# Cross-attention of a decoder layer: keys and queries interleaved by head, context in four buffers, stacks not cleared

## The reference

```python
q = (x @ Wq).reshape(B, N, HEADS, hd).transpose(0, 2, 1, 3)        # HEADS 16, hd 32
k = (context @ Wk).reshape(B, M, HEADS, hd).transpose(0, 2, 1, 3)
v = (context @ Wv).reshape(B, M, HEADS, hd).transpose(0, 2, 1, 3)
scores = jnp.einsum('bhid,bhjd->bhij', q, k) * scale
scores = jnp.where(context_mask[:, None, None, :], scores, max_neg)
attn = jax.nn.softmax(scores, axis=-1)
out = jnp.einsum('bhij,bhjd->bhid', attn, v)
return out.transpose(0, 2, 1, 3).reshape(B, N, DIM) @ Wo
```

## Time and profile before

| | |
|---|---|
| median of 3 runs | 4101.87 us |
| the profiled execution | 4104.39 us |
| its span | 4102.5 us |
| PE busy | 3330.3 us (81%) |
| DVE busy | 2647.3 us (65%) |
| ACT busy | 2227.0 us (54%) |
| POOL busy | 1061.0 us (26%) |
| DMA packets | 582.43 MB, mean 142 GB/s |

### The profile page before, as it was taken

The page is one execution under the profiler, slowest core; times in us unless marked ns, Lnnn a source line. Parts: engine busy times, 40 slices in busy tenths (PEclk is TensorE's granted clock), DMA queues, the critical chain, the costliest instruction groups (busy, mean ns, idle before and its releaser), DMA issues. The chain is left out here.

```text
span 4102.5 us, 50439 instructions
## 1 busy us (share of the span) xinstructions
PE 3330.3 (81%) x15064; PEld 2553.6 (62%) x15064; DVE 2647.3 (65%) x4397; ACT 2227.0 (54%) x4058; POOL 1061.0 (26%) x1139
## 2 busy tenths in 40 slices
PE   5899999999999996377877778775729989950799
PEld 4687877777787875244554455543518877740587
DVE  5787777777777774555655566565653349977554
ACT  4676767667676763155655555563122224448665
POOL 1233333232323232044544444453300000000000
PEclk9999999999999998688988898897969999985899
DMA  4444443444434432333333333324642237779775
GB/s 128 127 131 124 139 123 124 131 134 120 133 120 129 131 108 70 88 96 93 75 88 91 91 80 87 92 61 162 227 141 92 110 118 265 273 279 410 245 247 194
DMA packets 294941, 582.43 MB, mean 142 GB/s; under 512 B 37672, under 2 KB 119600, under 8 KB 280384
## 3 DMA queue, kind: packets, MB, share of 16 engines
q1 hardware_dynamic: 282048, 554.61, 42.6%
q10 hardware_dynamic: 12672, 25.17, 1.7%
HBM read 339.49 MB, written 172.79 MB: 125 GB/s over the span
## 5 line engine op out<-in xcount | busy, mean ns | idle before, releaser
L1555 DVE TENSOR_REDUCE ca_negm<-ca_mx 128x1 fp32r<-128x512 f32 x512 | 353.2, 690 | 433.2 <-PE ca_mx L1701 426.1
L640 POOL TENSOR_SCALAR sa_ex<-sa_ex,sa_rs 128x512 f32<-128x512 f32 x512 | 356.7, 697 | 952.3 <-DVE sa_rs L518 952.3
L513 DVE TENSOR_REDUCE sa_nm<-sa_st 128x1 f32<-128x512 f32 x512 | 351.1, 686 | 269.3 <-PE sa_st L747 268.2
L704 PE MATMUL sa_pj<-sa_xh,sa_w 128*128 128x512 f32 x1536 | 459.7, 419 | 11.7 <-DVE sa_kl L496 9.8
L389 ACT ACTIVATE sa_eh<-sa_tr 128x512 fp32r<-128x512 f32 x512 | 306.7, 599 | 293.9 <-PE sa_tr L757 290.8
L1628 POOL TENSOR_TENSOR ca_el<-ca_ex,ca_eh 128x512 fp32r<-128x512 f32 x256 | 365.5, 1429 | 164.8 <-ACT ca_eh L1484 163.9
L382 ACT ACTIVATE sa_ex<-sa_st,sa_nm 128x512 f32<-128x512 f32 x512 | 351.2, 686 | 58.2 <-DVE sa_nm L513 54.9
L522 DVE TENSOR_TENSOR sa_el<-sa_tr,sa_eh 128x512 fp32r<-128x512 f32 x512 | 351.2, 686 | 36.9 <-ACT sa_eh L389 30.1
L1476 ACT ACTIVATE ca_ex<-ca_st 128x512 f32<-128x512 f32 x512 | 298.2, 589 | 79.2 <-PE ca_st L1719 78.1
L1731 PE MATMUL ca_ov<-ca_eh,ca_vc 128*66 128x512 f32 x512 | 226.7, 443 | 120.0 <-ACT ca_osb L1491 72.2
L757 PE MATMUL sa_tr<-top_ident,sa_ex 128*128 128x128 f32 x2048 | 309.7, 274 | 0.2 <-POOL sa_ex L640 0.2
(11 more groups left out here) (244 smaller groups left out, 7695.9 us busy)
## 6 DMA issues: line engine op xcount, KB each, us to landing
sa_w<-w_split SPq DMA_DIRECT2D x56, 1536.0 KB, 7.4
up_g<-gate SPq DMA_DIRECT2D x50, 512.0 KB, 4.4
gate<-gate_ev SPq DMA_DIRECT2D x24, 1024.0 KB, 3.8
gate<-up_g SPq DMA_DIRECT2D x48, 512.0 KB, 2.9
up<-up_ev SPq DMA_DIRECT2D x24, 1024.0 KB, 5.6
mul_a<-gate SPq DMA_DIRECT2D x48, 512.0 KB, 12.0
mul_b<-up SPq DMA_DIRECT2D x48, 512.0 KB, 13.0
dn_a<-gate SPq DMA_DIRECT2D x96, 256.0 KB, 3.5
```

Of the source, the lines that this page charges most:

```text
L513: nc.vector.tensor_reduce(nm[:, u % U:u % U + 1], st[:, u % 2], AX_X, ALU.max, negate=True).then_inc(dve_mx, 1)
L640: nc.gpsimd.tensor_scalar(ex[:, u % U], ex[:, u % U], rs[:, u % U:u % U + 1], 1.0, ALU.mult, ALU.mult).then_inc(pool_n, 1)
L704: yield nc.tensor.matmul(pj[:, bank], w[:, n % 2, m, part, k], xx[:, b % 2, k], start=(i == 0 and k == 0), stop=(i == 2 and k == DK - 1))
L1555: nc.vector.tensor_reduce(negm[:, n % 2, qt, h:h + 1], mx[:, m % 2], AX_X, ALU.max, negate=True).then_inc(dve_mx, 1)
```

## The change

Five things, all in the cross-attention stage. (1) The columns of Wq and Wk are permuted within each group when they are split, so that the projection leaves element d of head j on partition 4d + j instead of 32j + d; the four heads of a group then go to their four stacks in one DMA, since partition 4d + j is written to partition d, head j. (2) Keys and queries, mask row and maxima need 8 DMAs a step instead of 32; all of a stack's DMAs count on one semaphore for each place of the ring, and keys are no longer issued at t = 5 and 7 but all at t = 8. (3) Context has four buffers and is loaded at t = 1 of the step before the one that transposes it. (4) The mask of the next batch is loaded before its x. (5) The rings are not cleared; POOL sets the rows of ones, and DVE sets the two columns of ones in vc alone.

```diff
+    STACKS = 16 * 7
-        cr = sp.sb("cr", [P, 2, CD])
+        cr = sp.sb("cr", [P, NT, CD])
+        def columns(tile, n):
+            if CK <= n < 2 * CK:
+                return tile
+            return tile.rearrange("p (g j d) -> p g d j", j=HS, d=XD)
+        def split_columns(tile, n):
+            if CK <= n < 2 * CK:
+                return tile
+            return tile.rearrange("p (g d j) -> p g d j", j=HS, d=XD)
             def load_context(j):
-                if j >= 2:
-                    e.wait_ge(pe_ct, j - 1)
-                e.dma_start(cr[:, j % 2], xs[j]).then_inc(cr_in[j % 2], 16)
+                if j >= NT:
+                    e.wait_ge(pe_ct, j - NT + 1)
+                e.dma_start(cr[:, j % NT], xs[j]).then_inc(cr_in[j % NT], 16)
+            def stack(n, tile, src, part):
+                e.dma_start(f32(tile[part * XD:(part + 1) * XD, n % RING]), f32(src[:, :])
+                            ).then_inc(stacked[n % RING], 16)
+            def stack_keys(n):
+                r = n % RING
                 if n >= RING:
                     e.wait_ge(pe_st, U * (n - RING) + U)
-                for j in range(HS):
-                    e.dma_start(f32(k4[MR:MR + 1, r, j]), env["mask_n"][b:b + 1, :]).then_inc(mask_in[r], 16)
+                e.dma_start(f32(k4[MR:MR + 1, r]), env["mask_n"][n // XG:n // XG + 1, :].partition_broadcast(HS)).then_inc(stacked[r], 16)
+                e.wait_ge(act_kh, n + 1)
+                stack(n, k4, kh, 0)
+                stack(n, k4, kh, 1)
+                e.wait_ge(pool_kl, n + 1)
+                stack(n, k4, kl, 2)
+            def stack_queries(n):
+                e.wait_ge(act_qh, n + 1)
+                stack(n, q4, qh, 0)
+                stack(n, q4, qh, 2)
+                e.wait_ge(dve_ql, n + 1)
+                stack(n, q4, ql, 1)
             def max_rows(n):
                 e.wait_ge(act_mr, n + 1)
-                for j in range(HS):
-                    e.dma_start(f32(q4[MR + 1:MR + 2, n % RING, j]), f32(mrow[j:j + 1, :])).then_inc(mr_in[n % RING], 16)
+                e.dma_start(f32(q4[MR + 1:MR + 2, n % RING]), f32(mrow[:, :])
+                            ).then_inc(mr_in[n % RING], 16)
...
-                if t == 5 and n < N:
-                    stack_keys(n, range(3), 0)
-                    stack_keys(n, range(3), 1)
-                if t == 7 and n < N:
-                    stack_keys(n, range(3), 2)
                 if t == 8 and n < N:
-                    for part in range(3):
-                        stack_keys(n, range(3, 4), part)
-                    mask_row(n)
-                    for j in range(HS):
-                        stack_queries(n, j)
-                if t == 3 and s >= 0 and s % XG == 1 and s // XG + 1 < B:
-                    load_context(NT * (s // XG + 1))
-                    load_context(NT * (s // XG + 1) + 1)
-                if t in (8, 10) and context_tile(s, t - 1) is not None:
-                    load_context(context_tile(s, t - 1) + 1)
+                    stack_keys(n)
+                    stack_queries(n)
+                if t == 1 and s >= 0 and s % XG == 0 and s // XG + 1 < B:
+                    for i in range(NT):
+                        load_context(NT * (s // XG + 1) + i)
                 if t == 9 and s >= 0 and s % XG == 1 and s // XG + 1 < B:
+                    load_mask(s // XG + 1)
                     load_x(s // XG + 1)
-                    load_mask(s // XG + 1)
...
-                nc.scalar.activation(w_hi[:, n], w_raw[:, n % 2], ACT.Copy).then_inc(act_w, 1)
+                nc.scalar.activation(split_columns(w_hi[:, n], n), columns(w_raw[:, n % 2], n), ACT.Copy).then_inc(act_w, 1)
...
-            nc.vector.memset(f32(q4[:]), 0.0).then_inc(zeroed, 1)
-            nc.vector.memset(f32(k4[:]), 0.0).then_inc(zeroed, 1)
-            e.wait_ge(zeroed, 2)
-            nc.vector.memset(f32(q4[MR:MR + 2]), 1.0).then_inc(zeroed, 1)
-            nc.vector.memset(f32(k4[MR:MR + 2]), 1.0).then_inc(zeroed, 1)
-            nc.vector.memset(f32(vc[:]), 1.0).then_inc(zeroed, 1)
+            nc.vector.memset(f32(vc[:, :, :, :, 2 * XD:VW]), 1.0).then_inc(ones_set, 1)
...
+            nc.gpsimd.memset(f32(q4[MR:MR + 2]), 1.0).then_inc(ones_set, 1)
+            nc.gpsimd.memset(f32(k4[MR:MR + 2]), 1.0).then_inc(ones_set, 1)
```

More of the change, by code:

```diff
@@ L42 @@
 WQMAX = 7.0
-ZEROED = 5
+ONES = 3
 BIG = float(2.0 ** 100)
@@ L1273, in cross_attention_stage @@
         dve_w = sp.sem("dve_w")
-        zeroed = sp.sem("zeroed")
-        cr_in = [sp.sem(f"cr_in{i}") for i in range(2)]
+        ones_set = sp.sem("ones_set")
+        cr_in = [sp.sem(f"cr_in{i}") for i in range(NT)]
         xq_in = sp.sem("xq_in")
@@ L1290, in cross_attention_stage @@
         dve_vl = sp.sem("dve_vl")
-        stacked = [[sp.sem(f"stacked{r}{j}") for j in range(HS)] for r in range(RING)]
-        mask_in = [sp.sem(f"mask_in{r}") for r in range(RING)]
+        stacked = [sp.sem(f"stacked{r}") for r in range(RING)]
         pe_mx = sp.sem("pe_mx")
@@ L1358, in load_mask @@
                 e.dma_start(maskb[:, :], env["mask_f"][b:b + 1, :].partition_broadcast(P)).then_inc(maskb_in, 16)
-            def stack_keys(n, heads, part):
+            def stack(n, tile, src, part):
+                e.dma_start(f32(tile[part * XD:(part + 1) * XD, n % RING]), f32(src[:, :])
+                            ).then_inc(stacked[n % RING], 16)
+            def stack_keys(n):
                 r = n % RING
[L1362 to L1371, removed]
@@ L1399, in outputs @@
                             ).then_inc(o_out[j % 2], 16)
-            for i in range(2):
-                load_context(i)
+            load_context(0)
             load_weights(0)
             load_weights(1)
-            for i in range(2, NT):
+            for i in range(1, NT):
                 load_context(i)
@@ L1412, in _ @@
                 load_weights(n)
-            e.wait_ge(zeroed, ZEROED)
+            e.wait_ge(ones_set, ONES)
             for G, s, t in slots():
@@ L1451, in high_key @@
                 if n:
-                    for j in range(HS):
-                        e.wait_ge(stacked[(n - 1) % RING][j], 96 * ((n - 1) // RING) + 96)
+                    e.wait_ge(stacked[(n - 1) % RING], STACKS * ((n - 1) // RING) + STACKS)
                 nc.scalar.activation(kh[:, :], km[:, :], ACT.Copy).then_inc(act_kh, 1)
@@ L1654, in transpose_context @@
                 bank_free()
-                e.wait_ge(cr_in[j % 2], 16 * (j // 2) + 16)
+                e.wait_ge(cr_in[j % NT], 16 * (j // NT) + 16)
                 if j % NT == 0 and j:
@@ L1659, in transpose_context @@
                 for k in range(CK):
-                    last = nc.tensor.transpose(ms[:, cols(k)], cr[:, j % 2, cols(k)], ident[:, :])
+                    last = nc.tensor.transpose(ms[:, cols(k)], cr[:, j % NT, cols(k)], ident[:, :])
                 last.then_inc(pe_ct, 1)
@@ L1715, in scores @@
                 if a % U == 0:
-                    e.wait_ge(mr_in[r], 64 * (n // RING) + 64)
+                    e.wait_ge(mr_in[r], 16 * (n // RING) + 16)
                 if a >= 2:
```

19 lines of the change are left out of this document (4 added, 15 removed).

## The result

The changed kernel takes 3908.72 us (median of 4 runs, 3906.31 to 3914.25), the kernel before, on the same chip, 4103.49 us: ratio 0.9525, 95% interval 0.9509 to 0.9542. The forecast was 3852 us in a range of 3800 to 3940: the side and the range are right, the gain is 195 us where 250 were forecast. The profiled run of the changed kernel took 3914.25 us, its span 3912.2.

What follows compares the result with a forecast made beforehand. No engine was full in cross-attention; waits from SP's issue order bound it. Profiled 4104.4 - 241 (steps) + 28 (x behind stacks) - 37 (start) = 3854, adjusted for a profiled run 2.5 us above the median: 3852 us, range 3800 to 3940.

Steps and rivals of the forecast that it cites:

- The start: Start of cross-attention: no clearing, earlier weight splits, faster first stacks and maxima together save 37 us.
- the 5.4 us of the first fill: Start of the stage: first stacks start once kh is there, flow 6.9 us, land by about 1722, saving 5.4 us.
- The strided weight reads: Weight splits of seven tiles, read with a step of 32 elements: 0 to 9.2 us lost, 2 taken.
- rival B: Weight splits: reading with a step costs four times the duration, giving 3878 us; chance 0.09.
- The context stall: Context steps: PE's 130.2 us of waits for tiles go when loaded a step ahead; such steps become 26.6 us.
- all of them move 227: Stack block in each step: all DMA engines move 227 GB/s, so six stacks, 1.57 MB, take 6.9 us.
- the cover of 0.7 us: Store of t = 12 behind the stacks: lands at 1898.5, ACT wants its buffer at 1899.2, so 0.7 us spare.
- the term of 4 us: Steps that load mask and x behind the stacks: 4 us lost in each of 7, 28 us in all.
- an ordinary step becomes 29.3 - 4.6 = 24.7 us: Ordinary cross-attention steps: ACT's wait of 4.6 us for the store goes, leaving 24.7 us (bounds 22.1 and 29.3).
- the forecast's signs: Cross-attention windows: steps of 24 to 26 us expected; forecast wrong if ordinary steps stay above 27 us.
- A: Store of t = 12: its wait moves from SP's issue into the DMA engines, costing 105, 3957 us; chance 0.13.
- C: Every step's stacks: the fused DMA falls on few engines, making the kernel slower, 4288 us; chance 0.05.

Runs made afterwards that it cites:

- micro: Also written (1): no layer computed, only copies in blocks of 1.57 MB, each awaited; six fused stacks took 11.7 us a block, 134 GB/s.
- keys7: Keys' stacks issued at t = 7 instead of t = 8, against the changed kernel with four output buffers and x ahead of the stacks: 3893.29 us, 0.9491.

## Why the prediction came out as it did

**The start: 33.9 for 37, in part by two misses that cancel.** DVE's first low part comes at 1648.04 (forecast: before 1652), PE's first projection at 1674.37 (near 1677), and putting the clearing back costs 34 us. The projection is 33.0 us earlier, where 29.5 were forecast (the first high part of a weight is itself 3.3 us earlier). What failed is the 5.4 us of the first fill: none of it came. The stacks leave SP by 1684, but the last lands 11 us after its issue: the same drain rate as in the steps. The maxima in one issue gave about 1.3 us for 1.9 (the first maximum tile is 32.6 us earlier, the next step's maxima 33.9).

**The strided weight reads: right.** 1.09 instead of 0.63 us on ACT, 1.05 instead of 0.69 on DVE, 1.7 and 1.5 times, inside the bounds of 1 and 2; rival B, at four times, is out. The Trainium skill's penalty for accesses that leave a 16-byte line (SBUF — State Buffer, section "Door 1: The DMA port swizzle") would give such a cost, and the trace agrees; the cost is small here.

**The context stall: right in its mechanism.** No wait of PE for a context tile is left, and loading it as before costs 84 us.

**The step that failed is "all of them move 227": six fused stacks take 11.7 us, not 6.9.** The forecast read the rate off single stacks at a share of 0.41 and scaled it to a full share. Copies of 128 partitions into 32 are slower in themselves: 134 GB/s alone (1), 137 to 143 in the kernel. By the forecast's own arithmetic the cover of 0.7 us at the store of t = 12 then becomes a lack of 4.1 us. It showed fully in the steps with x: there ACT waits 8.8 to 9.8 us and PE 3.4 to 4.3 for x, and the step takes 32.8 us against 25.9 in the fastest version, so the term of 4 us was in truth 7. The step behind it takes 28.0 us against 26.1, at a granted clock of 0.92 to 0.95, another 1.9. In the steps just ahead of those with x ACT waits 2.3 to 3.2 us, and they take 25.8 against 23.8. In the others it waits 1.1 us or not at all (3.0 and 3.5 at the end of the stage). In one of these, the step at 1799, 17.9 us lie between the end of the copy of t = 8 and the time at which ACT wants the buffer, where the forecast counted 15.6: this longer stretch is part of the cover, the rest I did not settle.

**The second step that failed, a smaller one, is "an ordinary step becomes 29.3 - 4.6 = 24.7 us".** It takes ACT's wait out of the mean and leaves out PE, the next to bound the step: the forecast's own row has PE busy for 26.68 of 28.70 us in one. Of three ordinary steps two don't come below 26.05 us in the mean of any version (PE busy 25.0, clock 1.00), the third comes down to 23.8; that is 25.3 in the mean of the three. In the changed kernel their mean is 26.6 us, above the 24 to 26 of the forecast's signs and below the 27 from which it called itself wrong.

**The sizes.** Four steps were to take 3 x 24.7 + 26.6 + 4 = 104.7 us; they took 112.45. Times 7.25 (29 steps) that is the 56 us missing in the steps. With four output buffers, x ahead of the stacks and stacks in pairs they take 101.72, against 100.7 forecast without a loss at x. That this is within 1% is in part luck: two steps are 1.4 us longer each than forecast, one is 0.9 shorter, and the one with x takes 25.6 to 26.3 for 26.6. What the queue behind the stacks costs, the clock with it, is 112.45 - 101.72 = 10.7 us in four steps where 4 were counted; that is 49 of the 56 us. The other 7 are the net of the misses just named.

**The rivals.** A (the wait moves into the DMA engines) was the right doubt, with the right place and the right reason, "if the block flows slower", and came in part: the missing 57 us, most of them from there, are a little over half of its 105. It deserved more than 0.13, since the forecast named a cover of 0.7 us and rested it on a rate that no row showed at a full share. C is out: fused stacks run on 16 engines (share 1.08). That is also what the Trainium skill's rule on the number of engines (DMA: Bandwidth & Descriptors, section "Why a DMA increments its semaphore by 16 and not by 1") gave; but 16 busy engines did not mean the rate of 16.

## What to carry to other kernels

Fewer, larger DMAs take time off the queue that issues them and put a block in front of everything behind it: work out the block's drain time from a row of the same shape at a full share, or measure the shape alone, and then ask what stands behind it in the queue. Put the transfer that is wanted first ahead of the block (32 us here; splitting its wait gave nothing that can be told), and choose the shape by its rate: two heads in a DMA beat four, though it takes twice the issues. A stall that goes was cover for others, so a single edit gives less than its stall (88 us, where PE had waited 130.2). And ask which engine bounds the step once the stall is gone: its busy time is the least that the step can take.

## What the runs showed of the hardware that was not expected

- Copies inside SBUF from one queue with all 16 engines busy, in rows of 2 KB, flow at rates that differ threefold by shape: 128 partitions to 128, 382 GB/s; 32 to 32 or to 128, 177 to 179; 64 to 32, 163; 128 to 64, 138; 128 to 32, 126 to 134.
- SP can be held in an issue. With the stacks, mask and x outstanding one small store took 5.68 us to issue, 4.9 to 6.8 over the 7 steps with x (3.42 in keys7), against 0.45 to 0.6 in ordinary steps. Six stacks alone did not bring it on: the store right behind them in micro took 0.54 us to issue. What fills up was not isolated.
- A memset of 2 x 6144 on POOL took 5.21 us, as long as one of 128 x 6144 on DVE (5.18); the forecast's upper bound had been 9.8.
- A store of 64 rows of 2 KB, alone, took 3.6 us by its packets, where the forecast's two engines gave 2.6; behind six stacks it took 2.7 more than they (14.4 for 11.7).
